# Routed experts on sorted rows instead of on every row, in a decoder layer on one core

## The reference

```python
x = x + attn(layernorm(x))           # 16 heads; causal Toeplitz mixing of the values
x = x + xattn(layernorm(x), ctx)     # queries from x, keys and values from ctx, causal softmax
x = x + ffn(layernorm(x))
```

```python
out = shared experts: 2 of width 128, on every row
probs = softmax(flat @ router_w)                  # 16 routed experts
weights, indices = top_k(probs, 2)                # normalised to sum 1
comb[t, e] = weight of expert e for row t, zero for 14 of 16
h = silu(flat @ wg_r[e]) * (flat @ wu_r[e])       # width 64 each
out += sum over e of comb[t, e] * (h @ wd_r[e])
```

## Time and profile before

| | |
|---|---|
| median of 3 runs | 673.53 us (673.47 to 674.89) |
| span of the profiled execution | 672.6 us |
| a run beside that span | 673.5 us, 0.9 us around the span |
| iteration 2 starts (its first router matmul) | 105.4 us |
| iterations 3 to 8 start | 180.4, 253.7, 327.0, 400.3, 473.5, 546.9 us |
| iteration 9 starts | 616.9 us |
| PE busy, instructions | 582.0 us (87%), 5212 |
| DVE, ACT, POOL busy | 486.3, 222.8, 198.2 us |

### The profile page before, as it was taken

The page is one execution under the profiler, slowest core; times in us unless marked ns, Lnnn a source line. Parts: engine busy times, 40 slices in busy tenths (PEclk is TensorE's granted clock), DMA queues, the critical chain, the costliest instruction groups (busy, mean ns, idle before and its releaser), DMA issues. The chain is left out here.

```text
span 672.6 us, 14191 instructions
## 1 busy us (share of the span) xinstructions
PE 582.0 (87%) x5212; PEld 389.0 (58%) x5212; DVE 486.3 (72%) x1133; ACT 222.8 (33%) x446; POOL 198.2 (29%) x221
## 2 busy tenths in 40 slices
PE   3338648998999899989999899989998989998796
PEld 2226426665775568556866567556855666665353
DVE  4656355868887788778787888788777867787574
ACT  3343113342334333442433333433334223322121
POOL 4312022225232342343322533234233320232132
PEclk9769576999999999999999999999999999999899
DMA  5887010391009500680029200860158002300500
GB/s 155 289 261 250 32 31 5 76 312 54 32 4 257 180 0 33 138 275 26 33 59 303 77 14 21 229 208 0 36 120 258 1 33 63 65 1 32 121 7 33
DMA packets 57201, 69.36 MB, mean 103 GB/s; under 512 B 2384, under 2 KB 46288, under 8 KB 56912
## 3 DMA queue, kind: packets, MB, share of 16 engines
q1 hardware_dynamic: 57168, 68.92, 35.8%
HBM read 64.13 MB, written 4.78 MB: 102 GB/s over the span
## 5 line engine op out<-in xcount | busy, mean ns | idle before, releaser
L464 POOL TENSOR_TENSOR mid<-gated,mid 128x512 f16<-128x512 f32 x80 | 95.0, 1188 | 196.6 <-ACT mid L589 196.6
L129 PE MATMUL wide<-w_d,mid 128*128 128x256 f16 x320 | 87.5, 273 | 4.7 <-POOL mid L464 4.1
L584 ACT ACTIVATE gated<-score 128x512 f32<-128x512 f32 x80 | 47.6, 595 | 129.1 <-PE score L131 115.2
L131 PE MATMUL wide<-w_d,mid 128*128 128x256 f16 x320 | 87.2, 273 | 0.0
L130 PE MATMUL wide<-w_d,mid 128*128 128x256 f16 x320 | 87.2, 273 | 0.0
L769 DVE TENSOR_TENSOR gated<-gated,stage 128x512 f32<-128x512 f32 x64 | 78.2, 1222 | 4.1 <-DMA stage<-comb_scratch 1.5
L763 DVE SCALAR_TENSOR_TENSOR gated<-gated,score 128x512 f32<-128x512 f32 x80 | 54.6, 682 | 33.4 <-ACT gated L584 32.2
L129 PE MATMUL rows<-h3T,w_gu 128*128 128x512 f16 x160 | 61.3, 383 | 12.9 <-DVE gated L772 11.7
L129 PE MATMUL score<-h3T,w_gu 128*128 128x512 f16 x160 | 60.9, 381 | 1.0 <-DVEq L109 1.0
L130 PE MATMUL rows<-h3T,w_gu 128*128 128x512 f16 x160 | 61.1, 382 | 0.0
L131 PE MATMUL rows<-h3T,w_gu 128*128 128x512 f16 x160 | 61.0, 381 | 0.0
(11 more groups left out here) (173 smaller groups left out, 1392.4 us busy)
## 6 DMA issues: line engine op xcount, KB each, us to landing
toep<-z_scratch SPq DMA_DIRECT2D x16, 2048.0 KB, 15.8
stage<-comb_scratch SPq DMA_DIRECT2D x32, 512.0 KB, 7.6
x_in<-in_x SPq DMA_DIRECT2D x8, 512.0 KB, 13.1
cT_in<-in_ctxT SPq DMA_DIRECT2D x8, 512.0 KB, 3.5
out<-x_out SPq DMA_DIRECT2D x8, 512.0 KB, 3.0
stage<-in_gu_r SPq DMA_DIRECT2D x1, 2048.0 KB, 11.1
stage<-in_wd_r SPq DMA_DIRECT2D x1, 1024.0 KB, 13.3
x_out<-in_gu_s SPq DMA_DIRECT2D x1, 512.0 KB, 6.3
```

The lines of the kernel that those rows point to most:

```text
L129: pe.matmul(out, stationary[0], moving[0], start=start, stop=False, **kw)
L131: return pe.matmul(out, stationary[1], moving[0], start=False, stop=stop, **kw)
L464: pool.tensor_tensor(mid[:, 1, j % SLOTS], gated[:, j % SLOTS], mid[:, 0, j % SLOTS], ALU.subtract).then_inc(mid_split.sem, 1)
L584: act.activation(gated[:, j % SLOTS], score.bank(f"g{j}")[:], ACT.Tanh, scale=0.5 / (X_H * X_W)).then_inc(tanh_done.sem, 1)
```

## The change

The routed experts no longer run on every row. For each batch the row's two experts are known after `route`; a mask matmul (`count_before`) counts, for every row and choice, how many rows before it chose the same expert, and so gives each of the 1024 row-choices of a batch a place in a DRAM tensor that has one region for each expert. POOL writes the rows there with 8 indirect transfers of 128 rows (`scatter`). Four batches make a group. When the last batch of a group is placed (iterations 5 and 9), DVE makes a table of tiles of 128 rows (`tabulate`), POOL zeroes what follows each expert's rows with 8 more indirect transfers (`fill_tails`), PE turns the table, and every quad of four tiles (12 quads for a group) runs its expert matmuls, with the expert's number read from the table into registers. A quad takes three steps: turn and split the rows, gate and up, down. The 14 steps of a group stand at fixed points of the program (`SLOTS`): group 0 in iterations 6 (5 steps), 7 (5) and 8 (4), group 1 all at the end of iteration 9.

The results of the quads go to DRAM, tile by tile. After the last iteration's own work POOL fetches for each batch the two result rows of every row with 8 indirect transfers (`gather`, 32 for each group), DVE adds them with their weights to the rest of the layer's result, which was parked in DRAM, and SP stores the batch (`finish`, `store_out`). POOL issues the 32 fetches of group 0 in iteration 9 ahead of its part in group 1's steps.

Beside this: the loop is written out; ring buffers replace the lists of bank turns; the order of `scores`, `turn_probs`, `part_prob` is closer packed, with the bank of a score freed by ACT's exponential; `add_bias` and `part_mid` on POOL stand behind the scatter; the routed weights are split in eight pieces at the ends of iterations 1 to 4 and the down weights are loaded twice; 16 transfers of 256 KB write zeros to the spare rows before the rest of the weights is loaded.

```diff
+GROUPS = ((0, 1, 2, 3), (4, 5, 6, 7))
+QUADS = [-(-(TOP * len(batches) * C + NE - 1) // 4) for batches in GROUPS]
+SPARE = [(4 * QUADS[g] - TOP * ROOM[g] // P) * P for g in range(len(GROUPS))]
+RUN = 2
+PART = P * NE // P
+SLOTS = {
+    6: (1, 1, 1, 1, 1, 0),
+    7: (1, 1, 1, 1, 1, 0),
+    8: (1, 1, 1, 1, 0, 0),
+    9: (0, 0, 0, 0, 0, 14),
+}
...
@@ sync
+            def load_quad(g, q):
+                n = quad_no(g, q)
+                if q == 0:
+                    sp.wait_ge(tab_made.sem, g + 1)
+                    sp.wait_ge(scattered.sem, scattered.at(GROUPS[g][-1], 16 * C * TOP))
+                    sp.wait_ge(tail_filled.sem, tail_filled.at(g, 16 * (PART // RUN)))
+                    sp.wait_ge(spare_filled, sum(SPARE) // (P * RUN) * 16)
+                if n >= NX:
+                    sp.wait_ge(r_turned.sem, r_turned.at(n - NX, 1))
...
+                for t in range(4):
+                    sp.dma_start(r_x[:, n % NX, t], x_dram[bass.ds(at[t], P), :]).then_inc(r_loaded[n % NX].sem, 16)
+            def finish(b):
+                if b >= 2:
+                    sp.wait_ge(out_stored[b % 2], 16 * (b // 2))
...
+                sp.dma_start(x_out[b % 2][:], part_dram[b].rearrange("(c p) e -> p c e", p=P))\
+                    .then_inc(part_loaded[b % 2], 16)
+            finish(0)
+            finish(1)
+            for b in range(B):
+                store_out(b)
+                if b + 2 < B:
+                    finish(b + 2)
@@ gpsimd
+            def scatter(b):
+                pool.wait_ge(placed.sem, placed.at(b, 4))
+                for n in range(C * TOP):
+                    pool.indirect_dma_start(
+                        out=x_dram, out_offset=bass.IndirectOffsetOnAxis(ap=row_of[:, b, n:n + 1], axis=0),
+                        in_=h3[:, n // TOP], in_offset=None).then_inc(scattered.sem, 16)
...
+            for it in range(B + 2):
+                f, m, d, n = stages(it)
...
+                if m:
+                    reciprocal_deviation(it - 1, 1)
+                if d:
+                    scatter(it - 2)
+                    if it - 2 == GROUPS[GROUP_OF[it - 2]][-1]:
+                        fill_tails(GROUP_OF[it - 2])
+                if f and m:
+                    rows.wait_emptied(pool, (it, "o2"))
+                    add_bias(it)
+                slots(it, 0)
+                if d:
+                    part_mid(it - 2, 0)
+                    part_mid(it - 2, 1)
+                slots(it, 1)
...
+                if it == B + 1:
+                    for b in GROUPS[0][:NROW]:
+                        gather(b)
+                slots(it, 5)
+            for b in range(min(NROW, len(GROUPS[0])), B):
+                gather(b)
@@ tensor
+            def slots(it, point):
+                for g, s in SLOTS_AT.get((it, point), ()):
...
+                    if s >= 2:
+                        to = turned.bank(("mid", g, s - 2))[:].bitcast(F16)
+                        turned.fill(pe, ("mid", g, s - 2))
+                        pe.wait_ge(r_mid_split.sem, r_mid_split.at(n, 1))
+                        for t in range(4):
+                            last = pe.transpose(to[:, P * t:P * t + P], r_mid[:, n % 2, t].rearrange("p a m -> p (a m)"),
+                                                identh[:])
...
+                    if s < QUADS[g]:
+                        for half in range(2):
+                            turned.fill(pe, what)
+                            for t in range(2):
+                                for k in range(K2):
+                                    last = pe.transpose(turned.bank(what)[:, P * (K2 * t + k):P * (K2 * t + k) + P],
+                                                        r_x[:, n % NX, 2 * half + t, P * k:P * k + P], ident[:])
...
+                    if 1 <= s <= QUADS[g]:
+                        which = experts(g, s - 1)
+                        for t in range(4):
+                            for k in range(K2):
+                                w = [w_gur[:, a, k, bass.ds(which[t], 1), :].rearrange("p n m -> p (n m)")
+                                     for a in range(2)]
+                                last = three_passes(pe, to, [r_xT[:, n % 2, a, t, k] for a in range(2)], w,
+                                                    start=(k == 0), stop=(k == K2 - 1))
...
+                    if s >= 2:
+                        which = experts(g, s - 2)
+                        for half in range(2):
+                            rows.fill(pe, what)
+                            turned.wait_emptied(pe, ("mid", g, s - 2))
+                            for t in range(2):
+                                for a in range(2):
+                                    w = w_dr[:, a, bass.ds(which[2 * half + t], 1), :].rearrange("p n e -> p (n e)")
+                                    last = pe.matmul(rows.bank(what)[:, E * t:E * t + E], r_midT[:, n % 2, 2 * half + t],
+                                                     w, start=(a == 0), stop=(a == 1))
+                            last.then_inc(rows.is_filled(what), 1)
+                            rows.wait_filled(pe, what)
+                            pe.sem_inc(r_y_ready.sem, 1)
@@ vector
+            def finish(b):
...
+                for n in range(C * TOP):
...
+                    dve.scalar_tensor_tensor(to, y_rows[:, at + n], w_top[:, b, n % TOP, n // TOP:n // TOP + 1], to,
+                                             ALU.mult, ALU.add).then_inc(y_added.sem, 1)
```

More of the change, by code:

```diff
@@ L39 @@
 NEG = -1e30
-SLOTS = 3
 X_H = 256.0
@@ L73 @@
[L73 to L124, removed]
@@ new lines, with slots_by_point @@
+POINTS = 6
+SLOTS = {
[4 more added lines that the diff above has]
+}
+def slots_by_point():
+    steps = [(g, s) for g in range(len(GROUPS)) for s in range(QUADS[g] + 2)]
+    out, n = {}, 0
+    for it, counts in SLOTS.items():
+        for point, count in enumerate(counts):
+            out[it, point] = steps[n:n + count]
+            n += count
+    assert n == len(steps), (n, len(steps))
+    return out
+SLOTS_AT = slots_by_point()
@@ L264, in decoder_layer @@
[L264 to L269 removed]
+        stage_small = sb("stage_small", [P, 2 * K2 * H])
+        x_flat = x_res[:].rearrange("p n c e -> p (n c e)")
@@ L270, in decoder_layer, with ring @@
+        turned_order, score_order, rows_order = bank_orders()
+        def ring(name, order):
+            return Ring(order, [bank(f"{name}{k}") for k in range(2)], [sem(f"{name}_filled{k}") for k in range(2)],
+                        [sem(f"{name}_emptied{k}") for k in range(2)])
+        turned = ring("turned", turned_order)
+        score = ring("score", score_order)
+        rows = ring("rows", rows_order)
         wide = bank("wide", [P, 2, 512])
-        comb_dram = nc.dram_tensor("comb_scratch", [NE, S], F32, kind="Internal").ap()
@@ L388, in _ @@
                     load_context(0)
-            def iteration(it, f, m, d, n):
+            for it in range(B + 2):
+                f, m, d, n = stages(it)
                 if f:
@@ L651, in _ @@
+                if n:
+                    part_turned(it, h1T, h1T_hi, "h1", reverse=True)
+                if m:
+                    part_turned(it, h3T, h3T_hi, "h3")
+                if it in PIECES:
+                    part_weights(PIECES[it])
+                slots(it, 5)
         @block.vector
         def _(dve):
-            turned.begin(dve, turned.taken, "h1.0")
-            for banks in (score, rows):
-                dve.sem_inc(banks.taken.sem, len(banks.order))
-            for n in range(3):
-                dve.sem_inc(h_ready[n].sem, 1)
@@ L940, in _ @@
+                if m:
+                    part_turned(it, it - 1, h3T, h3T_hi, "h3")
+                if it in PIECES:
+                    part_weights(PIECES[it])
+                slots(it, 5)
+            for b in range(B):
+                finish(b)
         @block.tensor
         def _(pe):
-            turned.begin(pe, turned.ready, "h1.0")
-            for banks in (score, rows):
-                pe.sem_inc(banks.ready.sem, len(banks.order))
-            pe.sem_inc(q_ready.sem, 2)
-            pe.wait_ge(const_made, 9)
```

1335 lines of the change are left out of this document (861 added, 474 removed).

## The result

The changed kernel takes 862.59 us (median of 4, 861.75 to 863.00) against 674.14 (673.47 to 674.89): ratio 1.279, 95% interval 1.278 to 1.281. The forecast of 740 had the sign right and the size wrong; 862.6 lies above the upper end, 822.

The account below looks back on a forecast made before the run. PE bounds steady iterations before; afterwards the chain between engines does. Iteration 9 starts at 541.4, its third step at 598.8, twelve steps end at 688.8, plus 50 and 0.9: 740 us. Forecast 700 to 790 (0.42), wider range 655 to 822.

Parts of the forecast that it names:

- The start: Before iteration 2: toep 10.5 us late from added transfers, iteration 1 gains 4.5; iteration 2 starts at 111.4 instead of 105.4.
- With c = 1 the wait is 3.5 us and the iteration 52 us: Steady iteration without routed pairs: PE waits for POOL's split before `down(0)`, behind 8 indirect transfers; PE alone would need about 41.
- my own sign: Start of iteration 9, forecast at 541.4: the prediction is wrong if it comes after 560.
- rival (4): Tail in iteration 9 at half clock, quad steps of 11 us: 785 us, with more register work 822; chance 0.20.
- The price c: POOL's time to issue one indirect transfer: taken as 1.0 us, bounded by 0.35 and 1.51.
- Iterations 5 to 8: Iteration 5 has 8 us extra for tables; 6 and 7 take 74 us each with five 6.0 us steps; 8 takes 66.
- Alone, a step is ... 7.5: Iteration 9's tail: a quad step is a round through all engines, 6.9 us, 7.5 with register work; twelve take 90.
- Group 0's 32 fetches in the way: Iteration 9: 32 fetches, 32 us, stand before POOL's first split of the quads; third step starts at 598.8.
- Rivals (1) to (3): (1) c = 0.37, 692 us, chance 0.16; (2) quad step 3.9 us, 652, 0.14; (3) PE bounds everywhere, about 560, 0.05.

Follow-up runs that it names:

- quiet: One group of runs, four kernels side by side on one chip, without a kind of wait worth 17 to 24 us that every other run of a changed kernel has.

## Why the prediction was wrong

**The start** was right in mechanism: PE waited for toep until 57.16, 11.0 us later than before, forecast 10.5. But iteration 1 gained 11.4 us and not 4.5, so nothing was left of it at iteration 2. (The idle DMA time of the earlier trace rows around 12 to 17 us is 3.75 us in that stretch, not 4.5.)

**"With c = 1 the wait is 3.5 us and the iteration 52 us"** is the step that failed first. The wait is there, at its place, ended by POOL as described; it is 6.3 us, and the iteration 61.3. By my own sign, a start of iteration 9 after 560, the prediction was wrong: it was 612.7, not 541.4. Two things were mis-sized. The scatters cost 8.2 us of the period (61.3 against 52.6 to 53.5 without them), not 3.5; 2.2 us of that is c, at 1.27. And the chain without any scatter, which I counted at 48.5, is 53. A term for the clock was missing: the added matmuls show that at least 3.3 us of a 61.3 us iteration are lower clock. How the rest of the 9.3 us divides is open. I had used the half clock only for the tail, in rival (4), though the earlier trace rows showed 0.60 for iteration 1, which I had read myself as a chain that leaves PE idle.

**The price c.** Forecast 1.0 inside the bounds 0.35 to 1.51, measured start to start and averaged over a run of them 1.28 to 1.31 for scatters and tails, 1.25 to 1.26 for the 32 fetches in a row, 1.29 to 1.33 for those at the end. The difference is small and is multiplied often: by my own rule of some 8 us for each 0.1 it is, at 1.27, an estimated 22 of the 122 us. By the Trainium skill, page "DMA: Bandwidth & Descriptors", section "Anatomy of one DMA", generating descriptors is a small cost; here each transfer held POOL for 1.25 us or more, and the measurement decides.

**Iterations 5 to 8.** Five steps cost 24.7 to 27.6 us above the steady period, forecast 22; tails and tables in iteration 5 cost 13.4, forecast 8. That 8 was for the tables alone: the eight transfers that zero the tails there, 10.3 us of POOL (16 in a row from 312.90, 1.29 us each), were in no term of the sum. Mostly these lines inherit the 9 us of the steady period; 13.7 us in iterations 7 and 8 are the late signals (89.0 and 74.3, against 82.1 and 67.4 quiet).

**"Alone, a step is ... 7.5"** failed next: the steady step is 10.3, and the line of the tail is 33 us too long. Rival (4), to which I gave 0.20, named a part of the cause: half clock in the tail. It is shown by the added matmuls (clock 0.60 to 0.97, 12.7 us for the twelve, in spite of the 1.7 us of work they add to each). Its price was not right: it asked 3.35 us a step for the clock, and giving the clock back won 1.3. That its 11 us a step came near the 10.3 is luck as far as the clock goes. Of the other 1.5 us some 0.7 are the gate-up matmuls, priced at 1.3 us and 2.0 even at the full clock. The gap of 0.8 us ahead of them, which the profile puts down to DVE, is the same at either clock; by PE's program it holds the wait for its own last transposes and the reading of the expert numbers, and it stands against 0.6 for the unseen register work. That the tail is a round through all engines was right: with the clock up the step still is 9.0.

**Group 0's 32 fetches in the way** was right in mechanism: they took 40 us where 32 were forecast, and taking them out of the way gave 29.

**Not foreseen at all:** the signals that arrive only when POOL's run is over, 17 to 24 us, not to be read from a trace without such a run. Rivals (1) to (3) are out: c was not 0.37, the steady step was 10.3 us and not under 4.7, and the iterations took 61.3 us and not 41. The quiet changed kernel was not measured; the column suggests some 840, still outside the range. As an estimate from the parts, c (22), the clock where it was tested (9.9 in iterations 2 to 4, 12.7 in the tail) and the late signals (21.3) make 66 of the 122 us, if they don't overlap; the rest is in the chain that was counted too short and in the terms named above, and is not separated. The sign was forecast with its mechanism, a small gain per iteration and a long tail, but the gain was nearly nothing and the tail, from the start of iteration 9, 248 us instead of 197.

## What to carry to other kernels

Taking work from the engine that is the bound pays only down to the chain behind it, and on PE that chain is then walked at a lower clock: here 0.81 in the steady iterations and 0.60 in the tail. Give the clock a term in every stretch in which PE would wait, and don't count on all of it: idle matmuls won back 3.3 of 61.3 us and 1.3 of 10.3, and nothing in iterations where PE had the steps to do or where the scatters stood first. An indirect transfer from POOL is an instruction of 1.25 to 1.33 us in POOL's order; put a run of them where POOL waits anyhow and nobody waits for POOL, and not ahead of a split that PE needs: moving two such runs won 28 and 29 us, beside a loss of 188. If variants of one kernel are compared, run them side by side on one chip with the unaltered one among them.

## What the hardware showed unexpectedly

During POOL's runs of indirect transfers, on two of three chips and in the changed kernel's first runs, DVE, ACT and PE waited on though what they waited for was done, mostly until about the end of the run, at most 6.6 us longer, and sometimes to a point inside it. With the scatters first, the idle time so ended was 6.9 to 7.6 us of ACT in each of six iterations and 2.7 to 4.1 us of DVE in four; around the 32 fetches it was up to 21.3 us of ACT. These are whole idle times, of which the late signal is only the last part. The third chip showed none with the same program. With the rows stored by SP the waits are gone wherever POOL no longer scatters, outside iteration 9. What in the chip holds the signals back, and why not everywhere, is open and was not tried.
